# Attention of a graph network: a fourth probability chunk turned by DMA in heads 4 and 5, and the next tile's queries and mask fetched with heads 7, 0 to 3 and 5

## The chip, the cores and the metric

The kernel runs on one core of one Trainium2 chip. A core has TensorE (PE; its weight loads are listed as PEld), VectorE (DVE), ScalarE (ACT), GpSimd (POOL) and SyncE (SP), which here only issues DMAs. The metric is the time of one execution on the device, in microseconds; lower is better.

## What is computed

A graph convolution layer, then two transformer layers over the 2500 nodes, 40,000 edges, then a layer norm. The change lies in the attention of the two transformer layers:

```python
scores = jnp.einsum('ehd,ehd->eh', q[tgt], k[srcidx])
m = jax.ops.segment_max(scores, tgt, num_segments=n)
p = jnp.exp(scores - m[tgt])
s = jax.ops.segment_sum(p, tgt, num_segments=n)
w = p / (s[tgt] + 1e-16)
agg = jax.ops.segment_sum(w[:, :, None] * v[srcidx], tgt, num_segments=n)
attn = agg.reshape(n, D) @ Wo[l].T + bo[l]
x = _batchnorm(x + attn, g1[l], beta1[l])
```

n is 2500, D 512, with 8 heads of 64.

## The kernel before

The kernel does the sparse attention densely. A table `bias_rows` of 2500 x 2500 holds, for every pair of nodes, a mask or the logarithm of the number of edges, which is added to the score. The nodes are cut into 20 tiles of 125 target nodes. For each tile all 8 heads are worked, 160 units (tile, head) per layer, u = 8 * tile + head; the 2500 source nodes of a unit are 5 chunks of 500, k = 0 to 4.

For each chunk: PE makes the scores in PSUM (`score`, 2 matmuls of 500 columns, as the queries are kept in two fp16 halves). DVE adds the mask and keeps the chunk's maximum (`add_bias`); after five chunks it makes the unit's maximum (`maximum`, semaphore `maxed`). ACT takes the exponential in three pieces, chunks 0 and 1, chunks 2 and 3, chunk 4 (`exps`). Then the probabilities have to be turned so that source nodes lie on the partitions, and be cut into a high and a low fp16 half. There are two ways:

- By PE, chunks 1 and 3: 4 transposes in fp32 into a bank of `t_ps` (`turn_weights`), ACT copies the high half to `p_hi` (`high_half`), DVE subtracts to get `p_lo` (`low_half`).
- By DMA, chunks 0, 2 and 4 (`BY_DMA`): POOL (for chunk 4 ACT) copies the high half into a buffer `staged` (`high_to_stage`), POOL subtracts for the low half (`low_to_stage`), SP issues one DMA transpose of both halves into `across` (`turn`). There are 3 buffers `staged` (`STAGES`) and 4 `across` (`ACROSS`), used in the order of the chunks. A high half may be written only when the transpose of the chunk three before has landed (`crossed`), and a transpose may go out only when PE has used the chunk four before (`weighted`).

In both cases PE then multiplies with the values, 8 matmuls of 128 columns per chunk (`weigh`), three chunks behind the scores in its order. ACT and DVE read out the unit's sum (`read_high`, `read_low`).

The order of each engine is written out by hand, and each engine works it strictly in order. In its turn u of the loop PE does for k = 0 to 4: scores (u+2, k), transposes (u, k) if by PE, one piece of the tile's extra work (`EXTRA`), and `weigh` of the chunk three back. The extra work is that of the tile before: its sums transposed (heads 1 and 2) and the product with `wo`, two of four parts in head 3 and two in head 4. ACT does in turn u: `high_half(u, 1)`, `high_half(u, 3)`, `read_high(u-1)`, `exps(u+1, 0)` at k = 0, `(u+1, 1)` at k = 2, `(u+1, 2)` at k = 4, and right behind that `high_to_stage(u+1, 4)`. POOL goes through the DMA chunks only, and SP through their transposes. SP also fetches the next tile's 16-bit queries (two DMAs, one per half of the partitions, at head 0) and its mask (five chunks of columns, at heads 1 to 5), ahead of the transposes of the same head. DVE normalises the tile before at the end of its turn of head 0.

Of the kernel before, what the change touches and what calls it, by code (L numbers as in the profile page):

```python
# [86 lines left out]
ACROSS = 4  # L87

# [3 lines left out]
for u in range(UNITS):  # L92
    for k in range(NKC):
        if k in BY_PE:
# [1052 lines left out]
def attention(nc, sem, psum, sb, g, layer):  # L1147
# [6 lines left out]
    with ExitStack() as ctx:  # L1154
# [37 lines left out]
        high_staged = {k: sem(f"high_staged{k}") for k in BY_DMA}  # L1192
        low_staged = {k: sem(f"low_staged{k}") for k in BY_DMA}
# [15 lines left out]
        def pe_chunk(u, k):  # L1209
            return len(BY_PE) * (U0 + u) + BY_PE.index(k)  # L1210

        def dma_chunk(u, k):
            return len(BY_DMA) * (U0 + u) + BY_DMA.index(k)

        def dma_chunk_at(n):
            return n // len(BY_DMA), BY_DMA[n % len(BY_DMA)]

        def user_done(engine, n):

            if n < 0:  # L1220
                return
            in_layer, n = divmod(n, len(USERS))
            what, where, part = USERS[n]
            if what == "P":
                engine.wait_ge(bank_read, len(BY_PE) * (UNITS * in_layer + where) + BY_PE.index(part) + 1)
# [13 lines left out]
        def high_to_stage(engine, copy, u, k):  # L1239
            n = dma_chunk(u, k)  # L1240
            engine.wait_ge(stages_cleared, CLEARED * (layer + 1))
            if n >= STAGES:
                m = n - STAGES
                engine.wait_ge(crossed[m % ACROSS], 16 * (m // ACROSS + 1))
            apart(engine, g["waits_met"])
            for piece, (c0, c1) in enumerate(EXPS):
                if c0 <= k < c1:
                    engine.wait_ge(exped, len(EXPS) * (U0 + u) + piece + 1)
            copy(staged[n % STAGES][0:P, 0:BPC, 0:P],  # L1249
                 prob[u % PROBS][:, k * KC:(k + 1) * KC].rearrange("p (s c) -> p s c", s=BPC)).then_inc(high_staged[k], 1)  # L1250

        def low_to_stage(engine, u, k):
            here = staged[dma_chunk(u, k) % STAGES]
            engine.wait_ge(high_staged[k], U0 + u + 1)
            engine.tensor_tensor(here[0:P, BPC:2 * BPC, 0:P],  # L1255
                                 prob[u % PROBS][:, k * KC:(k + 1) * KC].rearrange("p (s c) -> p s c", s=BPC),
                                 here[0:P, 0:BPC, 0:P], ALU.subtract).then_inc(low_staged[k], 1)

        with nc.Block() as block:
            @block.sync  # L1260
            def _(sp):
                def load_queries(t):
                    for half in range(2):
                        sp.dma_start(queries_sb[t % 2][64 * half:64 * half + 64, 0:QW],
                                     q_tiles[t * DH:(t + 1) * DH, :]).then_inc(q_loaded[t % 2], 16)

                def load_mask(t, c):
                    at = slice(c * KC, (c + 1) * KC)
                    for p0, p1 in CUTS:
                        sp.dma_start(bias[t % 2][p0:p1, at], bias_rows[P * t + p0:P * t + p1, at]).then_inc(mask_loaded[t % 2], 16)  # L1270

                def turn(u, k):
                    n = dma_chunk(u, k)
                    if n >= ACROSS:
                        before, chunk = dma_chunk_at(n - ACROSS)
                        sp.wait_ge(weighted, NKC * before + chunk + 1)
                    sp.wait_ge(low_staged[k], U0 + u + 1)
                    apart(sp, g["waits_met"])
                    sp.dma_start_transpose(across[n % ACROSS][:, :, :], staged[n % STAGES][:, :, :].rearrange("p s c -> p (s c)")
                                           ).then_inc(crossed[n % ACROSS], 16)  # L1280

                load_queries(0)
                for c in range(NKC):
                    load_mask(0, c)
                for u in range(UNITS):
                    t, h = u // H + 1, u % H
                    if t < NT:

                        if h == 0:
                            if t > 1:  # L1290
                                sp.wait_ge(maxed, U0 + H * (t - 1))
                            load_queries(t)
                        if 0 < h <= NKC:
                            load_mask(t, h - 1)
                        if t == 1 and h == NKC + 1:
                            sp.dma_start(wo_sb[:, :, :].rearrange("p c d -> p (c d)"), g["wo"][layer * 128:(layer + 1) * 128, :]
                                         ).then_inc(wo_loaded, 16)
                    for k in BY_DMA:
                        turn(u, k)

            @block.gpsimd
            def _(pool):
# [7 lines left out]
                for u in range(UNITS):  # L1310
                    for k in BY_DMA:
                        if HIGH_BY[k] == "POOL":
                            high_to_stage(pool, pool.tensor_copy, u, k)
                        if LOW_BY[k] == "POOL":
                            low_to_stage(pool, u, k)

            @block.tensor
            def _(pe):
# [29 lines left out]
                def weigh(u, k):  # L1348
                    if k == 0:
                        reached(pe, agg_out, U0 + u - 1)  # L1350
                    if k in BY_PE:
# [44 lines left out]
                for u in range(UNITS):  # L1396
                    for k in range(NKC):
                        if u + 2 < UNITS:
                            score(u + 2, k)
                        if k in BY_PE:  # L1400
# [13 lines left out]
            def _(act):  # L1414
# [8 lines left out]
                def high_half(u, k):  # L1423
# [28 lines left out]
                for u in range(UNITS):  # L1452
                    for k in range(NKC):
                        if k in BY_PE:
# [15 lines left out]
            def _(dve):  # L1470
                def add_bias(u, c):
                    b = u // H % 2
                    if c == 0:
                        if u % H == 0:
                            dve.wait_ge(mask_loaded[b], BOTH * NKC * ((T0 + u // H) // 2 + 1))
                        for k in BY_DMA:
                            reached(dve, low_staged[k], U0 + u - PROBS + 1)
# [53 lines left out]
                def stage_lows(u, step):  # L1531

                    for k in BY_DMA:
                        if LOW_BY[k] == "DVE" and k + 2 == step:
                            low_to_stage(dve, u, k)

# [4 lines left out]
                for step in range(NKC):  # L1541
                    stage_lows(0, step)
                for u in range(UNITS):
                    for k in range(NKC):
                        if u + 2 < UNITS:
                            add_bias(u + 2, k)
                        if k in BY_PE:
# [324 lines left out]
```

## Time and profile before

| | us |
|---|---|
| median of 3 runs | 3387.66 |
| lowest, highest | 3385.79, 3404.86 |
| the profiled execution | 3393.12 |
| its span | 3391.3 |
| attention, layer 0 | about 1000 to 1962 |
| attention, layer 1 | about 2285 to 3245 |

The profile covers one execution. A line of the page or of a view says: line and engine, operation, what it writes and reads by the program's names (buffer numbers left out), shapes, count, busy time and mean ns of one, and the idle time ahead of it with what ended it. A timeline gives single instructions by start time. Matmuls are pipelined: one of 128 columns is shown with 0.22 us and the next starts 0.055 us later, so start times and not durations tell what PE spends.

### The profile page before, as it was taken

How to read it: one execution, taken by the hardware profiler on the slowest of the kernel's cores; microseconds unless marked ns; L12 is line 12 of the kernel's file. 1: busy time of each engine (PE TensorE's matmuls, PEld its weight loads, DVE VectorE, ACT ScalarE, POOL GpSimd, SP SyncE). 2: the span in 40 equal slices, each digit the busy share in tenths (PEclk: the TensorE clock that was granted, in tenths of full speed). 3: DMA queues.
4: the chain of work that ended last, by engine and by line, in shares of the span. 5: the costliest groups of instructions: out<-in, count | busy, mean ns of one | idle time of the engine just before them, and what ended most of it. 6: DMA issues, size and time to landing. Idle time of an engine off the chain costs nothing. (4 is left out here: it accounts for less than half of the span.)

```text
span 3391.3 us, 72342 instructions
## 1 busy us (share of the span) xinstructions
PE 2990.1 (88%) x24802; PEld 2279.6 (67%) x24802; DVE 2267.0 (67%) x6951; ACT 1965.5 (58%) x3918; POOL 2155.7 (64%) x1991
## 2 busy tenths in 40 slices
PE   2368999978869999999999989989999999999985
PEld 2124655645537778887787877757777778888874
DVE  8594334332337888888888853227888888888856
ACT  0123444433337788888787821227787788888834
POOL 1687877778617777777777710007777777777734
PEclk9999999988989999999999989999999999999998
DMA  9666666645579888888888831238898988888852
GB/s 372 102 126 157 125 122 130 114 91 92 99 194 171 168 166 170 170 175 175 162 167 174 156 84 25 52 72 177 166 166 166 174 171 171 168 173 173 162 120 61
DMA packets 1297462, 496.76 MB, mean 146 GB/s; under 512 B 1237240, under 2 KB 1262865, under 8 KB 1291408
## 3 DMA queue, kind: packets, MB, share of 16 engines
q1 hardware_dynamic: 1156197, 460.22, 63.7%
q0 software_dynamic: 133120, 0.80, 4.2%
q10 hardware_dynamic: 7788, 31.21, 2.8%
q8 instruction: 196, 3.21, 0.4%
q14 instruction: 161, 1.32, 0.1%
HBM read 153.55 MB, written 80.48 MB: 69 GB/s over the span
## 5 line engine op out<-in xcount | busy, mean ns | idle before, releaser
L1255 POOL TENSOR_TENSOR staged<-prob,staged 125x500 f16<-125x500 f32 x960 | 1071.3, 1122 | 166.0 <-ACT staged L1249 87.0
L1483 DVE CUSTOM_DVE_ANT_0 prob<-s_ps,mask 125x500 f32<-125x500 f32 x1600 | 1042.3, 673 | 179.5 <-PE s_ps L1333 116.2
L1420 ACT ACTIVATE prob<-prob,neg_max 125x1000 f32<-125x1000 f32 (+1 forms) x960 | 954.7, 994 | 58.9 <-DVE scrap L1489 53.8
L1333 PE MATMUL s_ps<-keys,queries 128*128 128x500 f16 x3200 | 945.7, 377 | 43.7 <-DMA queries<-q_tiles 28.0
L529 POOL DMA_INDIRECT counts<-count,cell x320 | 653.3, 2042 | 256.3 <-issue 98.1
L1361 PE MATMUL o_ps<-values,across 125*128 125x128 f16 x7680 | 586.8, 219 | 63.9 <-DMA across<-staged 63.4
L1361 PEld LDWEIGHTS o_ps<-values,across 125*128 125x128 f16 x7680 | 502.7, 97 | 200.8 <-issue 70.1
L1249 POOL CAST staged<-prob 125x500 f16<-125x500 f32 x640 | 385.5, 602 | 334.4 <-ACT prob L1420 201.6
L1496 DVE TENSOR_TENSOR p_lo<-t_ps,p_hi 125x500 f16<-125x500 f32 x640 | 434.4, 679 | 171.6 <-ACT p_hi L1430 167.2
L1430 ACT CAST p_hi<-t_ps 125x500 f16<-125x500 f32 x640 | 364.0, 569 | 146.3 <-PE t_ps L1344 145.0
L1344 PEld LDWEIGHTS t_ps<-identity,prob 125*125 125x125 f32 x2560 | 378.2, 188 | 92.0 <-ACT prob L1420 4.4
L1344 PE MATMUL t_ps<-identity,prob 125*125 125x125 f32 x2560 | 383.9, 272 | 2.7 <-ACT agg L1440 2.7
L1361 PE MATMUL o_ps<-values,p_hi 125*128 125x128 f16 x2560 | 355.6, 219 | 1.1 <-DVE p_lo L1496 1.1
L1361 PE MATMUL o_ps<-values,p_lo 125*128 125x128 f16 x2560 | 354.7, 219 | 0.0
L1249 ACT CAST staged<-prob 125x500 f16<-125x500 f32 x320 | 195.6, 611 | 202.9 <-issue 144.1
L1333 PEld LDWEIGHTS s_ps<-keys,queries 128*128 128x128 f16 x3200 | 249.7, 100 | 65.2 <-DVE chunk_max L1483 31.0
L1361 PEld LDWEIGHTS o_ps<-values,p_lo 125*128 125x128 f16 x2560 | 250.5, 98 | 26.8 <-issue 0.5
L1361 PEld LDWEIGHTS o_ps<-values,p_hi 125*128 125x128 f16 x2560 | 250.5, 98 | 25.8 <-DVE p_lo L1496 2.9
L1304 POOL MEMSET staged<- 128x1024 f16 x6 | 5.5, 951 | 381.0 <-POOLq L1053 307.8
L1383 PEld LDWEIGHTS t_ps<-agg,wo_sb 128*128 128x128 f32 x1280 | 169.9, 195 | 24.1 <-DVE p_lo L1496 2.1
L1420 ACT ACTIVATION_READ_ACCUMULATOR prob<-prob,neg_max 125x1 f32 x960 | 185.3, 193 | 0.0
L899 PE MATMUL agg_ps<-values,turned 125*125 125x512 f32 x400 | 180.9, 592 | 0.0
(162 smaller groups left out, 3684.2 us busy)
## 6 DMA issues: line engine op xcount, KB each, us to landing
mask<-bias_rows SPq DMA_DIRECT2D x200, 218.8 KB
counts<-xt ACTq DMA_DIRECT2D x8, 3054.0 KB, 37.2
keys<-counts SPq DMA_DIRECT2D x40, 546.9 KB
bias_rows<-edge_bias SPq DMA_DIRECT2D x20, 1093.8 KB
queries<-q_tiles SPq DMA_DIRECT2D x80, 250.0 KB, 3.9
pair_row<-pair_flat SPq DMA_DIRECT2D x40, 437.5 KB
across<-staged SPq DMA_TRANSPOSE x960, 3.0
q_tiles<-q_both SPq DMA_DIRECT2D x80, 125.0 KB, 3.0
```

What stands on the lines that cost most here:

```text
L529: pool.indirect_dma_start(counts, bass.IndirectOffsetOnAxis(cell[:, c:c + 1], 0), count[:, c:c + 1], None, compute_op=ALU.add).then_inc(gr ...
L899: mm = pe.matmul(agg_ps[t % 2][0:P, :], lhsT=turned_sb[u % 2][0:P, j * P:(j + 1) * P], rhs=hw(s), start=(s == 0), stop=(s == NT - 1))
L1249: copy(staged[n % STAGES][0:P, 0:BPC, 0:P], prob[u % PROBS][:, k * KC:(k + 1) * KC].rearrange("p (s c) -> p s c", s=BPC)).then_inc(high_st ...
L1255: engine.tensor_tensor(here[0:P, BPC:2 * BPC, 0:P], prob[u % PROBS][:, k * KC:(k + 1) * KC].rearrange("p (s c) -> p s c", s=BPC), here[0:P ...
L1333: mm = pe.matmul(s_ps[n % SB][:, 0:KC], lhsT=queries_sb[b][:, at:at + 128], rhs=keys[:, h, c * KC:(c + 1) * KC], start=(part == 0), stop=( ...
L1344: mm = pe.transpose(t_ps[r][0:P, s * P:(s + 1) * P], prob[u % PROBS][:, (k * BPC + s) * P:(k * BPC + s + 1) * P], identity[0:P, 0:P])
L1361: mm = pe.matmul(o_ps[u % 2][:, 0:2 * DH], lhsT=weights[:, s, :], rhs=values[:, u % H, k * BPC + s, :], start=(k == 0 and s == 0 and half ...
L1383: mm = pe.matmul(t_ps[r][:, 0:P], lhsT=wo_sb[:, k, o * 128:(o + 1) * 128], rhs=agg_t[t % 2][:, k * P:(k + 1) * P], start=(k == 0), stop=(k ...
L1420: act.activation(here, here, ACT.Exp, bias=neg_max[u % 4][:, :], accum_out=sums[u // H % 2][:, u % H, piece:piece + 1]).then_inc(exped, 1)
L1430: act.copy(p_hi[m % PB][:, :, 0:P], t_ps[r][0:P, 0:KC].rearrange("p (s c) -> p s c", s=BPC)).then_inc(p_high, 1)
L1483: dve.tensor_tensor_reduce(out=prob[u % PROBS][:, at], in0=s_ps[n % SB][0:P, 0:KC], in1=bias[b][:, at], scale=1.0, scalar=MASKED, op0=ALU. ...
L1496: dve.tensor_tensor(p_lo[m % PB][:, :, 0:P], t_ps[r][0:P, 0:KC].rearrange("p (s c) -> p s c", s=BPC), p_hi[m % PB][:, :, 0:P], ALU.subtrac ...
```

## The change

Heads 4 and 5 (`MORE_AT`) turn chunk 1 by DMA too, so that they have chunks 0, 1, 2 and 4 by DMA and only chunk 3 by PE. POOL makes both halves of chunk 1. The chunks are numbered through in two lists, `DMA_CHUNKS` and `PE_CHUNKS`, and the waits count by these; chunks 0 and 1 share one pair of semaphores. The number of buffers stays at 3 and 4. The next tile's fetches are spread anew: at head 7 of tile t, ahead of its transposes, SP waits for `maxed` and fetches the first half of the queries and mask chunk 0 of tile t + 2; then, in tile t + 1, the second half of the queries at head 0, mask chunks 1 to 3 at heads 1 to 3, and chunk 4 at head 5. The branch for low halves on DVE, which was not used, is gone. The core of the diff:

```diff
-BY_DMA = (0, 2, 4)
-BY_PE = tuple(k for k in range(NKC) if k not in BY_DMA)
-HIGH_BY = {0: "POOL", 2: "POOL", 4: "ACT"}
-LOW_BY = {0: "POOL", 2: "POOL", 4: "POOL"}
+MORE_AT = (4, 5)
+HIGH_BY = {0: "POOL", 1: "POOL", 2: "POOL", 4: "ACT"}
+STAGED_BY = {0: 0, 1: 0, 2: 2, 4: 4}
...
+def by_dma(u):
+    return (0, 1, 2, 4) if u % H in MORE_AT else (0, 2, 4)
...
                 def turn(u, k):
                     n = dma_chunk(u, k)
                     if n >= ACROSS:
-                        before, chunk = dma_chunk_at(n - ACROSS)
-                        sp.wait_ge(weighted, NKC * before + chunk + 1)
-                    sp.wait_ge(low_staged[k], U0 + u + 1)
+                        sp.wait_ge(weighted, weighted_by(DMA_CHUNKS, n - ACROSS))
+                    sp.wait_ge(low_staged[STAGED_BY[k]], staged_by(u, k))
...
-                load_queries(0)
+                def begin_next(t):
+                    if t < NT:
+                        if t > 1:
+                            sp.wait_ge(maxed, U0 + H * (t - 1))
+                        load_queries(t, 0)
+                        load_mask(t, 0)
+
+                def go_on(t, h):
+                    if t < NT:
+                        if h == 0:
+                            load_queries(t, 1)
+                        elif h <= 3:
+                            load_mask(t, h)
+                        elif h == 5:
+                            load_mask(t, 4)
+
+                for half in range(2):
+                    load_queries(0, half)
                 for c in range(NKC):
                     load_mask(0, c)
+                begin_next(1)
                 for u in range(UNITS):
-                    t, h = u // H + 1, u % H
-                    if t < NT:
-
-                        if h == 0:
-                            if t > 1:
-                                sp.wait_ge(maxed, U0 + H * (t - 1))
-                            load_queries(t)
-                        if 0 < h <= NKC:
-                            load_mask(t, h - 1)
-                        if t == 1 and h == NKC + 1:
...
-                    for k in BY_DMA:
+                    t, h = u // H, u % H
+                    if h == H - 1:
+                        begin_next(t + 2)
+                    else:
+                        go_on(t + 1, h)
+                    if t == 0 and h == NKC + 1:
...
+                    for k in by_dma(u):
                         turn(u, k)
```

## Rows read from the trace of the kernel before

**Rows 1.** Windows: stretch, us, busy (count) PE, PEld, DVE, ACT, POOL, PEclk, DMA share, GB/s.

```profile
1000.00:1962.00 962.00, 922.71 (x9867) 758.55 (x9865) 800.93 (x2579) 763.94 (x1625) 715.65 (x795) 0.99 0.85 167
2285.00:3245.00 960.00, 924.88 (x9934) 760.06 (x9934) 802.69 (x2586) 768.28 (x1637) 720.42 (x800) 1.00 0.86 168
1254.20:1302.04 47.84, 46.31 (x504) 38.37 (x502) 40.24 (x129) 38.83 (x83) 35.81 (x40) 1.00 0.88 172
1254.20:1260.88 6.68, 5.39 (x61) 4.26 (x59) 5.04 (x17) 5.10 (x12) 3.34 (x4) 1.00 1.10 217
...
1286.35:1291.58 5.23, 5.23 (x62) 4.24 (x60) 4.37 (x16) 4.06 (x9) 3.88 (x5) 1.00 0.72 131
```

**Rows 2.** Groups by line on PE, 1000 to 1962 us.

```profile
L1361 PE MATMUL o_ps<-values,across 125*128 125x128 f16 x3792 | 290.4, 219 | 33.4 <-DMA across<-staged 33.1
```

**Rows 3.** Timeline of PE: start us, us, line, out<-in, count; head 5 and later.

```profile
1289.82 0.60 PE L1344 MATMUL t_ps<-identity,prob 125*125 125x125 f32 x4
1290.26 0.61 PE L1361 MATMUL o_ps<-values,across 125*128 125x128 f16 x8
...
1293.31 0.22 PE L1361 MATMUL o_ps<-values,p_hi 125*128 125x128 f16 x1
...
1295.49 0.61 PE L1361 MATMUL o_ps<-values,across 125*128 125x128 f16 x8
...
1300.72 0.61 PE L1361 MATMUL o_ps<-values,across 125*128 125x128 f16 x8
...
1306.04 0.55 PE L1361 MATMUL o_ps<-values,across 125*128 125x128 f16 x7
```

**Rows 4.** Timeline of POOL, the same tile; in brackets the idle time before.

```profile
1277.15 0.60 POOL L1249 CAST staged<-prob 125x500 f16<-125x500 f32 x1 [1.93 <-ACT prob L1420]
1277.84 1.11 POOL L1255 TENSOR_TENSOR staged<-prob,staged 125x500 f16<-125x500 f32 x1
...
1281.95 0.60 POOL L1249 CAST staged<-prob 125x500 f16<-125x500 f32 x1 [0.22 <-issue]
...
1286.45 1.10 POOL L1255 TENSOR_TENSOR staged<-prob,staged 125x500 f16<-125x500 f32 x1 [0.98 <-ACT staged L1249]
1288.64 0.60 POOL L1249 CAST staged<-prob 125x500 f16<-125x500 f32 x1 [1.08 <-ACT prob L1420]
...
1294.56 1.11 POOL L1255 TENSOR_TENSOR staged<-prob,staged 125x500 f16<-125x500 f32 x1
```

**Rows 5.** Timeline of SP's DMA issues, the same tile (successive ones of a kind merged).

```profile
1279.02 4.31 SPq L1279 DMA_TRANSPOSE across<-staged  x3
1283.38 1.01 SPq L1270 DMA_DIRECT2D mask<-bias_rows  x2
...
1300.27 1.22 SPq L1264 DMA_DIRECT2D queries<-q_tiles  x2
```

**Rows 6.** Landing times of line L1279's transposes issued at 1279.0, 1284.5, 1301.7.

```profile
DMA to landing us min/median/max: 2.8/2.8/2.8
...
DMA to landing us min/median/max: 4.0/4.0/4.0
...
DMA to landing us min/median/max: 4.2/4.2/4.2
```

**Rows 7.** Timeline of ACT, the same tile.

```profile
1284.92 0.72 ACT L1420 ACTIVATE prob<-prob,neg_max 125x500 f32<-125x500 f32 x1
...
1285.77 0.61 ACT L1249 CAST staged<-prob 125x500 f16<-125x500 f32 x1
1286.72 1.13 ACT L1420 ACTIVATE prob<-prob,neg_max 125x1000 f32<-125x1000 f32 x1 [0.35 <-DVE scrap L1489]
...
1288.75 1.13 ACT L1420 ACTIVATE prob<-prob,neg_max 125x1000 f32<-125x1000 f32 x1
...
1290.46 0.58 ACT L1430 CAST p_hi<-t_ps 125x500 f16<-125x500 f32 x1 [0.49 <-PE t_ps L1344]
```

**Rows 8.** The page's groups, DVE's subtraction.

```profile
L1496 DVE TENSOR_TENSOR p_lo<-t_ps,p_hi 125x500 f16<-125x500 f32 x640 | 434.4, 679 | 171.6 <-ACT p_hi L1430 167.2
```

More of the change, by code:

```diff
@@ L87, with by_pe @@
 ACROSS = 4
+def by_dma(u):
+    return (0, 1, 2, 4) if u % H in MORE_AT else (0, 2, 4)
+def by_pe(u):
+    return tuple(k for k in range(NKC) if k not in by_dma(u))
+DMA_CHUNKS = [(u, k) for u in range(UNITS) for k in by_dma(u)]
+PE_CHUNKS = [(u, k) for u in range(UNITS) for k in by_pe(u)]
+DMA_AT = {chunk: n for n, chunk in enumerate(DMA_CHUNKS)}
+PE_AT = {chunk: n for n, chunk in enumerate(PE_CHUNKS)}
+STAGED_AT = {}
+for signal in (0, 2, 4):
+    for n, chunk in enumerate(c for c in DMA_CHUNKS if STAGED_BY[c[1]] == signal):
+        STAGED_AT[chunk] = n
+STAGED_COUNT = {signal: sum(STAGED_BY[k] == signal for u, k in DMA_CHUNKS) for signal in (0, 2, 4)}
 EXTRA = {(1, 4): ("T", 0), (2, 2): ("T", 1), (3, 2): ("O", 0), (3, 4): ("O", 1), (4, 2): ("O", 2), (4, 4): ("O", 3)}
@@ L93 @@
     for k in range(NKC):
-        if k in BY_PE:
+        if k in by_pe(u):
             USERS.append(("P", u, k))
@@ L1224, in user_done @@
             if what == "P":
-                engine.wait_ge(bank_read, len(BY_PE) * (UNITS * in_layer + where) + BY_PE.index(part) + 1)
+                engine.wait_ge(bank_read, len(PE_CHUNKS) * in_layer + PE_AT[where, part] + 1)
             elif what == "T":
@@ L1261, in _, with load_queries @@
             def _(sp):
[L1262 to L1265, printed above, removed]
+                def load_queries(t, half):
+                    sp.dma_start(queries_sb[t % 2][64 * half:64 * half + 64, 0:QW],
+                                 q_tiles[t * DH:(t + 1) * DH, :]).then_inc(q_loaded[t % 2], 16)
                 def load_mask(t, c):
@@ L1310, in _ @@
                 for u in range(UNITS):
-                    for k in BY_DMA:
+                    for k in by_dma(u):
                         if HIGH_BY[k] == "POOL":
                             high_to_stage(pool, pool.tensor_copy, u, k)
-                        if LOW_BY[k] == "POOL":
-                            low_to_stage(pool, u, k)
+                        low_to_stage(pool, u, k)
             @block.tensor
@@ L1475, in add_bias @@
                             dve.wait_ge(mask_loaded[b], BOTH * NKC * ((T0 + u // H) // 2 + 1))
-                        for k in BY_DMA:
-                            reached(dve, low_staged[k], U0 + u - PROBS + 1)
+                        if u >= PROBS:
+                            for k in by_dma(u - PROBS):
+                                dve.wait_ge(low_staged[STAGED_BY[k]], staged_by(u - PROBS, k))
+                        elif layer > 0:
+                            for signal in STAGED_COUNT:
+                                dve.wait_ge(low_staged[signal], STAGED_COUNT[signal] * layer)
                         apart(dve, g["waits_met"])
@@ L1529, in statistics @@
                                      xt[:, o, c * CH:(c + 1) * CH]).then_inc(bn_chunks, 1)
[L1531 to L1535, printed above, removed]
                 for u in range(2):
```

44 lines of the change are left out of this document (21 added, 23 removed).

## The prediction

> **Notation.** Chunk (h,k) is columns 500k to 500k+499 of head h's probabilities; (8,0) is head 0 of the next tile. A "unit" is one turn of the loop over heads. Times within the tile are written without their leading 1,2 or 1,3: 77.15 is 1277.15 us, 102.9 is 1302.9 us.
>
> **What bounds the kernel now.** I read first the busy times by stretch. The two attention stages hold 1922 us of the 3391 us span, and in them TensorE (PE) is busy 923 of 962 and 925 of 960 us, at the full granted clock [rows 1]. One tile of 8 heads takes 47.84 us with PE busy 46.31; nothing else in it comes near (DVE 40.24, ACT 38.83, POOL 35.81) [rows 1]. Then PE by line: of layer 0's idle time 33.4 us lie ahead of products with `across`, for 33.1 us of which the landing of a turned chunk is waited for [rows 2]. The windows say where: head 0 of the tile has 5.39 us of PE work in 6.68 us [rows 1], the rest being the wait for (0,0). So PE is the bound, and a second thing sits right behind it: the ring POOL copy, POOL subtract, SP issue, DMA landing, which has three `staged` buffers.
>
> How tight that ring is, the timeline of the engines in the tile 1254.20 to 1302.04 tells. A POOL chunk costs 0.60 + 1.11 us, with gaps 1.79 us from first start to end: 77.15, 77.84 + 1.11 = 78.95 [rows 4]. SP issues at 79.02 and needs about 1.3 us per transpose [rows 5]. It lands 2.8 us later when no fetch is near, 4.0 us later behind a mask's fetch, 4.2 us behind the queries' [rows 6]. A buffer's cycle is thus 1.79 + 0.08 + 2.8 + 0.14 = 4.8 us at best, for three chunks, against 5.23 us of PE time in a head without the product [rows 1].
>
> **Part 1: what is taken from PE.** In heads 4 and 5 the four fp32 transposes of chunk 1 go. They take 89.82 to 90.26 = 0.44 us of PE [rows 3]. Two per tile, 40 tiles: 80 x 0.44 = 35 us. The 8 products of the chunk stay, with `across` in place of `p_hi`/`p_lo`, at the same pitch. ACT loses one copy of 0.58 us, DVE one subtraction of 679 ns [rows 7, 8] per head, neither of which sets PE's time there: worth nothing by themselves.
>
> **Part 2: what is added.** Per such head POOL gets 1.79 us, SP one transpose of 1.3 us, the ring one more chunk. PE's shortening makes it worse: after both heads PE asks 0.88 us sooner. I follow the tile step by step, with the same durations.
> - (4,0): copy at 77.15 as now, subtracted 78.95, issued 79.0, landed 81.8.
> - (4,1), new: POOL 79.0 to 80.8. (4,2): to 82.7, issued 82.8, landed 85.6.
> - (4,4): ACT makes its high half, into the buffer of the chunk three before. That was (3,4), landed long ago; it is now (4,0), so ACT is held until 81.8 + 0.14 = 81.95 and its exponentials of head 5 end at 83.7 and 84.9. ACT has room here: it is waiting for PE anyway in this long unit, and exp (5,2) ends at 86.3 instead of 85.64 [rows 7]. POOL's half of (4,4) ends at 83.9, and SP may issue it at 84.1.
> - (5,0): POOL 83.95 to 85.75 (now 81.95 + 1.79 = 83.74 [rows 4]). SP: 84.1 + 1.23 + 1.01 for the mask of head 5 [rows 5] = 86.35; issue 86.4. It lands at 90.4 with the 4.0 us of its own row, at 89.2 with 2.8 us. PE reaches it at 90.26 - 0.88 = 89.4 [rows 3]: a stall of 0 to 1.0 us.
> - (5,4): ACT's high half stands in its queue ahead of the exponentials of head 6. The chunk three before is now (5,0), not (4,4). So ACT, which copies at 85.77 today [rows 7], is held until 89.35 to 90.55. Queued behind it: exp (6,0) and (6,1) at 1.13 us each and the copy of (5,3) at 0.58 us [rows 7], then DVE's subtraction at 0.68 us [rows 8]. Sum: 0.61 + 1.13 + 1.13 + 0.58 + 0.68 = 4.1 us, so `p_lo` of (5,3) is there at 93.5 to 94.7. PE wants it today at 93.31 [rows 3] and would after the change at 92.4. **Here the 0.88 us won are gone, and PE is 0.2 to 1.5 us later than today**, exp (6,0) at 91.1 to 92.3 against 87.85 is 3.2 to 4.4 us later.
>
> This hold is the step that I weigh most. DVE's bias adds and the next maximum also stand behind that subtraction.
>
> **Part 3: the fetches moved.** Mask 0 and half of the queries now stand ahead of (7,0) in SP's queue (1.01 + 0.6 us [rows 5]); the other half stays ahead of (8,0), which saves 0.6 us of issue there and some of the 4.2 us landing. The wait for `maxed` moved with them is for head 7's maximum, which ACT's exponentials needed before (7,0) could be staged: nothing, and queued behind it on SP is only (7,0). Head 4 is free of its mask (1.01 us of SP), which (4,0) uses. For the moved fetch alone: today (7,0) leaves POOL at 95.67 [rows 4], lands 4.0 us after its issue (as long as (5,0)'s) [rows 6], so at 99.7, and is reached at 100.72 [rows 3]: 1 us to spare; 1.6 us more of SP eats that, and (8,0) then waits for the buffer of (7,0). Gain and loss are about even.
>
> Together: exp (6,0) late by 3.2 to 4.4 us sets POOL to (6,0) at 91.2 to 92.4 instead of 88.64 [rows 4]; POOL then runs without a break, (6,0), (6,2), its half of (6,4), and ends (7,0) at 97.8 to 99.1. SP issues (6,4) at 96.0 to 97.5, then the fetch: (7,0) goes out at 98.9 to 100.4, lands at 101.7 (2.8 us) to 104.6 (4.2 us). PE gets it 1.1 to 4.0 us later than 100.72. (8,0) takes its buffer: +0.14 + 1.79 + 0.08 + 2.8 to 3.6 us of landing = 106.6 to 110.3, against 106.04 today [rows 3]. **One tile: +0.6 to +4.3 us.** I take +3.1, nearer the upper end, since (5,0) has the mask just ahead of it as its 4.0 us row has, and (7,0) a fetch as large as the one of the 4.2 us row; off the end, as each PE stall gives POOL and ACT time. With 38 tiles that have both parts: 38 x 3.1 = +118 us.
>
> The Trainium skill, Perfetto Trace Analysis, Optimization Strategy, says that the same gap repeating on the engine that should be full can mean too few buffers; the 33.1 us of waits for `across`, most of them for (0,0), agree. By it a fourth chunk in a three-buffer ring costs rather than saves; it gives no figure of its own.
>
> **The sum.** The profiled execution took 3393.1 us (span 3391.3), 5.5 above the median 3387.66. 3393 + 118 = 3511, on the median's scale 3505 us.
>
> **The rivals.**
> 1. *The relief is paid out (faster).* ACT's hold is short because (5,0) lands earlier than I say: it decides at 85.7, when ACT comes to the copy today; every landing before about 88.5 leaves (5,3) on time. Then 35 us are won, and if halving the queries' fetch also ends the waits for (0,0), at most 33 us per layer [rows 2], of which DVE at 40.24 of 47.84 us lets perhaps half through: 3388 - 35 - 30 = 3323, or 3353 without it. For it: PE is busiest by far. Against it: POOL has six full chunks and two halves to do between 77.15 and (5,4)'s end. Chance 0.15. The Trainium skill, Perfetto Trace Analysis, Identifying the Most-Contended Engine, would have the busiest engine relieved first, and so sides with this.
> 2. *POOL alone matters (even).* ACT's hold hides in PE's waits, and only POOL's 3.6 us per tile tell, of which its idle time today before (5,4) and (6,0) (0.98 + 1.08 us [rows 4]) takes 2.1. The remaining 1.5 us and PE's 0.88 stand against 2.2 us by which (6,0) is early today (POOL ends it at 88.64 + 1.79 = 90.43 [rows 4], landed 93.3 with 2.8 us, reached at 95.49 [rows 3]); the fetch ahead of (7,0) takes the gain back. -0.9 to +0.9 us per tile, centre 3390. Chance 0.22.
> 3. *The forecast*, chance 0.63, own range 3411 (+0.6) to 3551 (+4.3).
>
> **From cases to numbers.** A measurement of this kernel tells about 1% from no change: bounds 3354 and 3422. Faster: rival 1 with few exceptions, 0.15. Within 1%: rival 2 and the forecast's lowest edge, 0.23. Slower: 0.62. The range runs from 3370 (cutting off rival 1's 0.15) to 3560.
>
> **What would show it.** In the changed trace: POOL busy up by 80 x 1.7 = 137 us, transposes x1040, PE's t_ps<-identity,prob x2240. ACT's idle time ahead of `staged` on ACT, with (5,0)'s landing as what ends it, some 4 us per tile in head 5: the hold. PE then waits for DVE `p_lo` (today 0) and for `across` in heads 7 and 0. I am wrong in Part 2 if ACT's copy of (5,4) starts within 2 us of the end of exp (5,2), and in Part 3 if (7,0) lands in under 3.2 us.

## The result and the profile after

| | us |
|---|---|
| median of 3 runs | 3519.86 |
| lowest, highest | 3510.33, 3522.35 |
| the profiled execution, its span | 3510.33, 3508.1 |
| ratio to before, 95% interval | 1.0382 [1.0354, 1.0409] |

The change makes the kernel slower by 132 us, 3.8%. The page of the changed kernel, its busy times and three groups (columns as before: count, then busy us and mean ns, then the idle time just ahead and what ended it):

```profile
PE 2998.6 (85%) x24482; PEld 2234.0 (64%) x24482; DVE 2221.0 (63%) x6871; ACT 1901.7 (54%) x3838; POOL 2280.7 (65%) x2151
...
L1397 PE MATMUL o_ps<-values,across 125*128 125x128 f16 x8320 | 638.4, 219 | 148.1 <-DMA across<-staged 146.5
...
L1380 PE MATMUL t_ps<-identity,prob 125*125 125x125 f32 x2240 | 337.1, 273 | 3.7 <-ACT agg L1475 3.5
...
L1274 ACT CAST staged<-prob 125x500 f16<-125x500 f32 x320 | 195.6, 611 | 493.6 <-issue 434.0
```

The fp32 transposes are gone as meant (2240), and the 640 products moved to `across` are there (8320). But the wait for `across` has grown: 146.5 us in the whole span, where the kernel before has 63.4 (33.1 of it in layer 0, [rows 2]). ACT's copies into `staged` show the same thing: ACT stood idle ahead of them for 434.0 us of "issue", against 144.1 before. "Issue" is idle time for which the view names no releaser; in the tile below such a wait ends just behind the landing that frees the buffer.

```profile
L1249 ACT CAST staged<-prob 125x500 f16<-125x500 f32 x320 | 195.6, 611 | 202.9 <-issue 144.1
```

Of the 116.8 us by which the span grew, PE's waits for a landing take 83.1, those for DVE's maximum 22.5 (15.5 to 38.0), those for `p_lo` 9.5 (1.1 to 10.6): 115 us. PE's busy time should have fallen by 35 us and rose by 8.5. Part of that is how a busy PE is counted: eight products that stand alone are shown with 0.61 us [rows 3], while in a row they take 8 x 0.055 = 0.44, so every wait costs about 0.17 us more than the idle time shown; 140 more waits of these three kinds make 24 us. The other 20 us are open.

**Where it happens** is read from the windows of one tile, 1352.26 to 1403.36, here the whole tile and its heads 4, 5, 6 and 7 (columns as in [rows 1]):

```profile
1352.26:1403.36 51.10, 46.81 (x495) 37.09 (x493) 38.52 (x127) 36.76 (x80) 39.33 (x45) 1.00 0.89 171
1377.30:1383.87 6.57, 6.57 (x74) 5.67 (x72) 3.95 (x16) 4.01 (x9) 4.84 (x6) 1.00 0.71 141
1383.87:1388.84 4.97, 4.96 (x57) 3.66 (x55) 3.85 (x16) 1.47 (x4) 3.54 (x5) 1.00 0.84 193
1388.84:1396.06 7.22, 6.20 (x62) 4.08 (x59) 4.10 (x14) 6.31 (x15) 6.57 (x9) 1.00 0.68 141
1396.06:1403.36 7.30, 5.57 (x59) 4.27 (x59) 5.69 (x19) 5.73 (x14) 4.00 (x6) 1.00 1.14 205
```

The same four heads of before:

```profile
1279.34:1286.35 7.01, 7.01 (x78) 6.19 (x75) 5.05 (x16) 5.40 (x11) 5.67 (x7) 1.00 0.89 195
1286.35:1291.58 5.23, 5.23 (x62) 4.24 (x60) 4.37 (x16) 4.06 (x9) 3.88 (x5) 1.00 0.72 131
1291.58:1296.81 5.23, 5.23 (x62) 4.24 (x60) 4.73 (x16) 4.81 (x11) 4.45 (x6) 1.00 0.75 155
1296.81:1302.04 5.23, 5.23 (x62) 4.25 (x60) 4.64 (x16) 4.81 (x11) 3.81 (x5) 1.00 1.07 163
```

Head 4 wins exactly its 0.44 us (7.01 to 6.57). Head 5 wins 0.26. Then heads 6 and 7, which the change leaves alone but for the fetch, lose 1.99 and 2.07 us. Heads 0 to 3 take 25.04 us against 25.14. So the tile is 3.26 us longer (51.10 against 47.84), and all of its loss lies in heads 6 and 7, behind the change. The granted clock is full on both sides.

One tile is one case. The averages of 36 tiles of each trace (18 per layer, without the first and the last; a head is counted from its first matmul of scores to that of the next head) say how far it is typical, in us. The runs e1 to e9 are described below:

| | 0 | 1 | 2 | 3 | 4 | 5 | 6 | 7 | tile |
|---|---|---|---|---|---|---|---|---|---|
| before | 6.21 | 6.04 | 5.57 | 7.40 | 7.01 | 5.23 | 5.23 | 5.30 | 48.00 |
| the change | 5.60 | 6.43 | 5.75 | 7.14 | 6.57 | 5.56 | 7.12 | 6.89 | 51.05 |
| e1_fetch_only | 5.34 | 6.67 | 5.54 | 7.19 | 7.01 | 5.23 | 5.23 | 6.26 | 48.48 |
| e2_chunk_only | 7.16 | 5.90 | 5.83 | 7.12 | 6.58 | 5.79 | 7.13 | 5.66 | 51.17 |
| e4_before_4buf | 5.72 | 6.13 | 5.44 | 7.06 | 7.00 | 5.23 | 5.23 | 5.23 | 47.05 |
| e3_after_4buf | 5.52 | 6.29 | 5.45 | 7.02 | 6.57 | 5.01 | 5.95 | 6.34 | 48.15 |
| e9_less7 | 5.26 | 6.88 | 5.53 | 7.11 | 7.00 | 5.23 | 5.23 | 5.66 | 47.91 |

The tile shown is typical in heads 4, 6 and 7. In head 5 it is a lucky one: on average that head loses 0.33 us.

ACT in that tile, heads 4 and 5 (idle time before in brackets):

```profile
1379.86 0.61 ACT L1274 CAST staged<-prob 125x500 f16<-125x500 f32 x1 [3.18 <-issue]
...
1383.17 0.71 ACT L1456 ACTIVATE prob<-prob,neg_max 125x500 f32<-125x500 f32 x1
...
1387.47 0.61 ACT L1274 CAST staged<-prob 125x500 f16<-125x500 f32 x1 [3.50 <-issue]
1387.99 1.12 ACT L1456 ACTIVATE prob<-prob,neg_max 125x1000 f32<-125x1000 f32 x1
...
1390.22 0.55 ACT L1465 CAST p_hi<-t_ps 125x500 f16<-125x500 f32 x1
```

SP, which sends the transposes and the moved fetches:

```profile
1395.66 0.58 SPq L1288 DMA_DIRECT2D queries<-q_tiles  x1
1396.29 1.02 SPq L1294 DMA_DIRECT2D mask<-bias_rows  x2
1397.44 4.10 SPq L1302 DMA_TRANSPOSE across<-staged  x3
```

And PE:

```profile
1389.76 0.62 PE L1397 MATMUL o_ps<-values,across 125*128 125x128 f16 x8 [0.33 <-DMA across<-staged]
...
1391.55 0.23 PE L1397 MATMUL o_ps<-values,p_hi 125*128 125x128 f16 x1 [0.31 <-DVE p_lo L1535]
...
1402.05 0.61 PE L1397 MATMUL o_ps<-values,across 125*128 125x128 f16 x8 [1.71 <-DMA across<-staged]
```

ACT comes to the copy of (5,4) at 1383.97 and gets its buffer at 1387.47, 0.11 us after the landing of (5,0) (issued 1384.16, 3.2 us). Queued behind it are the exponentials of head 6 and the high half of (5,3), so PE gets `p_lo` of (5,3) late at 1391.55. POOL starts on head 6 late, at 1389.27, and then has only one break, of 0.40 us, before (7,0). SP sends (7,0) behind the fetch at 1397.44, it lands 4.5 us later, and PE stands 1.71 us for it.

### The profile page after: what moved, and what is told of

It reads as the page before. It is cut to its first block and busy times, and to the rows that moved or that the text cites. A ratio compares the mean times of both kernels' runs of the same rounds, so it can differ in the third digit from the quotient of the medians.

```text
span 3508.1 us, 71820 instructions
## 1 busy us (share of the span) xinstructions
PE 2998.6 (85%) x24482; PEld 2234.0 (64%) x24482; DVE 2221.0 (63%) x6871; ACT 1901.7 (54%) x3838; POOL 2280.7 (65%) x2151
## 5 line engine op out<-in xcount | busy, mean ns | idle before, releaser
L1280 POOL TENSOR_TENSOR staged<-prob,staged 125x500 f16<-125x500 f32 x1040 | 1149.9, 1110 | 214.4 <-ACT staged L1274 129.7
L1397 PE MATMUL o_ps<-values,across 125*128 125x128 f16 x8320 | 638.4, 219 | 148.1 <-DMA across<-staged 146.5
L1397 PEld LDWEIGHTS o_ps<-values,across 125*128 125x128 f16 x8320 | 537.3, 98 | 323.0 <-issue 118.5
L1274 POOL CAST staged<-prob 125x500 f16<-125x500 f32 x720 | 434.8, 604 | 287.1 <-ACT prob L1456 186.0
L1535 DVE TENSOR_TENSOR p_lo<-t_ps,p_hi 125x500 f16<-125x500 f32 x560 | 380.1, 679 | 307.2 <-ACT p_hi L1465 306.1
L1274 ACT CAST staged<-prob 125x500 f16<-125x500 f32 x320 | 195.6, 611 | 493.6 <-issue 434.0
L1380 PEld LDWEIGHTS t_ps<-identity,prob 125*125 125x125 f32 x2240 | 331.7, 188 | 82.8 <-ACT prob L1456 5.9
L1465 ACT CAST p_hi<-t_ps 125x500 f16<-125x500 f32 x560 | 315.9, 564 | 61.5 <-PE t_ps L1380 60.4
L1380 PE MATMUL t_ps<-identity,prob 125*125 125x125 f32 x2240 | 337.1, 273 | 3.7 <-ACT agg L1475 3.5
L1397 PE MATMUL o_ps<-values,p_hi 125*128 125x128 f16 x2240 | 312.6, 220 | 11.3 <-DVE p_lo L1535 10.6
L1397 PE MATMUL o_ps<-values,p_lo 125*128 125x128 f16 x2240 | 311.3, 219 | 0.0
```

The costliest lines, as they stand in the source:

```text
L1274: copy(staged[n % STAGES][0:P, 0:BPC, 0:P], prob[u % PROBS][:, k * KC:(k + 1) * KC].rearrange("p (s c) -> p s c", s=BPC)).then_inc(high_st ...
L1280: engine.tensor_tensor(here[0:P, BPC:2 * BPC, 0:P], prob[u % PROBS][:, k * KC:(k + 1) * KC].rearrange("p (s c) -> p s c", s=BPC), here[0:P ...
L1380: mm = pe.transpose(t_ps[r][0:P, s * P:(s + 1) * P], prob[u % PROBS][:, (k * BPC + s) * P:(k * BPC + s + 1) * P], identity[0:P, 0:P])
L1397: mm = pe.matmul(o_ps[u % 2][:, 0:2 * DH], lhsT=weights[:, s, :], rhs=values[:, u % H, k * BPC + s, :], start=(k == 0 and s == 0 and half ...
L1465: act.copy(p_hi[m % PB][:, :, 0:P], t_ps[r][0:P, 0:KC].rearrange("p (s c) -> p s c", s=BPC)).then_inc(p_high, 1)
L1535: dve.tensor_tensor(p_lo[m % PB][:, :, 0:P], t_ps[r][0:P, 0:KC].rearrange("p (s c) -> p s c", s=BPC), p_hi[m % PB][:, :, 0:P], ALU.subtrac ...
```

## The experiments

A ratio is always to the kernel before on the same chip; there that kernel took 3374 to 3378 us, and 3387.66 in the first row. The column "buffers" gives those of `staged`. "Old fetches" in an edit means SP's fetches as in the kernel before:

```diff
-                begin_next(1)
...
-                    if h == H - 1:
-                        begin_next(t + 2)
-                    else:
-                        go_on(t + 1, h)
+                    if t + 1 < NT:
+                        if h == 0:
+                            if t > 0:
+                                sp.wait_ge(maxed, U0 + H * t)
+                            load_queries(t + 1, 0)
+                            load_queries(t + 1, 1)
+                        if 0 < h <= NKC:
+                            load_mask(t + 1, h - 1)
```

| run | chunks by DMA per tile | buffers, fetches | us | ratio [95%] |
|---|---|---|---|---|
| the change | 26 | 3, new | 3519.86 | 1.0382 [1.0354, 1.0409] |
| e1_fetch_only | 24 | 3, new | 3407.57 | 1.0095 [1.0072, 1.0119] |
| e2_chunk_only | 26 | 3, old | 3519.95 | 1.0419 [1.0399, 1.0439] |
| e5_act_later | 26 | 3, new | 3525.75 | 1.0444 [1.0421, 1.0466] |
| e3_after_4buf | 26 | 4, new | 3395.79 | 1.0066 [1.0043, 1.0089] |
| e4_before_4buf | 24 | 4, old | 3347.20 | 0.9919 [0.9887, 0.9951] |
| e6_no_pool | 26 | 3, new | 3524.88 | 1.0449 [1.0419, 1.0480] |
| e7_stage4_across3 | 24 | 4 (`across` 3), old | 3385.57 | 1.0027 [1.0012, 1.0042] |
| e8_one_head | 25 | 3, old | 3452.33 | 1.0227 [1.0197, 1.0256] |
| e9_less7 | 23 | 3, old | 3385.49 | 1.0035 [1.0023, 1.0046] |
| e10_less7_newfetch | 23 | 3, new | 3407.35 | 1.0094 [1.0080, 1.0108] |
| e11_less0 | 23 | 3, old | 3416.77 | 1.0115 [1.0100, 1.0130] |
| e12_moved_chunk | 24 | 3, old | 3435.22 | 1.0166 [1.0148, 1.0184] |

### The two parts apart

e1_fetch_only, an edit to the changed kernel:

```diff
-MORE_AT = (4, 5)
+MORE_AT = ()
```

> The changed kernel with three DMA chunks in every head again; only the fetches stand where the change put them. Theory (ACT held at head 5's last chunk is the main loss, the moved fetch is about even by itself, since (7,0) had 1 us to spare and (0,0) gains what (7,0) loses): 3360 to 3410 us, ratio to before within 1%; PE's wait for the turned chunk moves from head 0 to head 7. Rival A (the fetch ahead of head 7 is the main loss, 1.6 us of PE waiting per tile there in the changed kernel): 3440 us or more. Rival B (the fetch move is a gain that the fourth chunk spoils): 3355 us or less.

e2_chunk_only is the changed kernel with the old fetches.

> The changed kernel with the queries and mask fetched at heads 0 to 5 as before; only the fourth chunk stays. Theory: the loss in heads 5 and 6 stays whole (PE idle 2.7 us there against 0.04), that of head 7 shrinks from 1.7 us to some 0.5, head 0's wait of 1 us comes back: +1 to +2 us per tile, 3425 to 3470 us. Rival A (the fetch is the main loss): 3355 to 3400 us, the relief of 35 us on PE showing at least in part. Additive effects would need e1 + e2 to sum to the change's +132 us; if they sum to less, the two make each other worse.

The fetch alone costs 0.95%, 31 us, and the chunks alone 4.2%: as much as both together. e2 is a miss; I had left a share of 50 to 90 us to the fetch. The groups of PE and the windows of a head 7 and the head 0 behind it in e1 tell what the fetch does:

```profile
L1397 PE MATMUL o_ps<-values,across 125*128 125x128 f16 x7680 | 587.9, 219 | 70.9 <-DMA across<-staged 69.9
L1369 PE MATMUL s_ps<-keys,queries 128*128 128x500 f16 x3200 | 945.4, 377 | 52.0 <-DMA queries<-q_tiles 27.0 <-DVE chunk_max L1522 24.4
...
2967.38:2973.38 6.00, 5.40 (x62) 4.26 (x60) 4.75 (x17) 4.87 (x12) 2.93 (x4) 1.00 1.08 237
2973.38:2978.60 5.22, 5.22 (x61) 4.24 (x59) 4.48 (x15) 4.43 (x9) 4.88 (x6) 1.00 0.70 170
```

Head 0, which took 6.68 us [rows 1], is down to 5.22. Head 7 is up from 5.23 to 6.00. The stall has moved from (8,0) to (7,0), and these two heads together lose nothing: on average head 7 is 0.96 us longer and head 0 is 0.87 shorter. What the fetch costs shows in head 1, which is 0.63 us longer. PE's waits altogether grew by 6.5 us for `across` and by 8.9 for DVE's maximum; these 15 us are half of the 31.

### Who is held: ACT, POOL or the ring

e5_act_later takes ACT's copy of (4,4) and (5,4) out of the way of the exponentials:

```diff
-                        if HIGH_BY[k] == "ACT" and step == min(k // 2 * 2 + 1, NKC - 1):
+                        if HIGH_BY[k] == "ACT" and u % H not in MORE_AT and step == min(k // 2 * 2 + 1, NKC - 1):
                             high_to_stage(act, act.copy, u, k)
...
+                        if k == 2 and u % H in MORE_AT:
+                            high_to_stage(act, act.copy, u, 4)
```

> The changed kernel, but in heads 4 and 5 ACT makes the high half of chunk 4 two steps later, behind the first two exponentials of the next head instead of ahead of them. No work or buffer is changed. Theory (the hold in ACT's queue): exponential (6,0) ends some 3 us earlier, PE's waits for p_lo and for DVE in head 6 (0.9 us per tile) go, and part of the wait in head 7: 1 to 2 us per tile, 3445 to 3480 us. Rival (POOL and the three-buffer ring by themselves bound heads 5 to 7, ACT's hold runs alongside): 3505 to 3530 us.

It gained nothing (1.0444). Its ACT timeline tells why, the copies of (5,4) and of (6,4):

```profile
3253.56 1.13 ACT L1456 ACTIVATE prob<-prob,neg_max 125x1000 f32<-125x1000 f32 x1 [0.99 <-DVE scrap L1530]
...
3256.66 0.61 ACT L1274 CAST staged<-prob 125x500 f16<-125x500 f32 x1 [0.76 <-ACT prob L1456]
...
3262.03 0.61 ACT L1274 CAST staged<-prob 125x500 f16<-125x500 f32 x1 [3.47 <-issue]
```

and its POOL timeline:

```profile
3257.35 1.10 POOL L1280 TENSOR_TENSOR staged<-prob,staged 125x500 f16<-125x500 f32 x1 [1.14 <-ACT staged L1274]
3258.39 0.60 POOL L1274 CAST staged<-prob 125x500 f16<-125x500 f32 x1
```

The exponential (6,0) is now done at 3254.69, as early as I wanted. But POOL takes up (6,0) only at 3258.39, since it makes its half of (5,4) first, and that waits for the same buffer: (5,0) lands at 3256.57, ACT copies (5,4) at 3256.66 and POOL follows at 3257.35. In head 6 ACT is held for 3.47 us, the hold of the changed kernel one head later. PE's waits for `across` stay (148.5 us). So the run does not free ACT everywhere (its idle time of "issue" ahead of `staged` is 318.9 us, against 434.0). What it shows is that an early exponential (6,0) alone gains nothing, since POOL then waits for the same buffer in its own queue.

e6_no_pool takes the new chunk's work from POOL: high half by ACT, low half by DVE.

```diff
-HIGH_BY = {0: "POOL", 1: "POOL", 2: "POOL", 4: "ACT"}
-STAGED_BY = {0: 0, 1: 0, 2: 2, 4: 4}
+HIGH_BY = {0: "POOL", 1: "ACT", 2: "POOL", 4: "ACT"}
+LOW_BY = {0: "POOL", 1: "DVE", 2: "POOL", 4: "POOL"}
+STAGED_BY = {0: 0, 1: 1, 2: 2, 4: 4}
...
-                        low_to_stage(pool, u, k)
+                        if LOW_BY[k] == "POOL":
+                            low_to_stage(pool, u, k)
...
-                        if HIGH_BY[k] == "ACT" and step == min(k // 2 * 2 + 1, NKC - 1):
+                        if HIGH_BY[k] == "ACT" and step == (3 if k == 1 else min(k // 2 * 2 + 1, NKC - 1)):
...
+                        if k == NKC - 1 and u + 1 < UNITS and 1 in by_dma(u + 1):
+                            low_to_stage(dve, u + 1, 1)
```

> The changed kernel, but chunk 1 of heads 4 and 5 gets its high half from ACT and its low half from DVE, which both have room there, so that POOL does what it did before the change; the three buffers and the order of the transposes stay. Ring theory (a buffer comes free only when the transpose three chunks before has landed, four chunks per head turn it 8 times in two heads): (4,4) still waits for (4,0) and (5,4) for (5,0), 0.2 to 0.5 us per tile better at most, 3490 to 3525 us. POOL theory (its 3.6 us more per tile): 3390 to 3430 us.

Its page:

```profile
PE 3001.3 (85%) x24482; PEld 2235.7 (64%) x24482; DVE 2270.3 (65%) x6951; ACT 1945.0 (55%) x3918; POOL 2165.9 (62%) x1991
```

POOL is back near its 2156 us of before (2165.9), and the time is 3524.88, so POOL's own work is not what costs. In e6 ACT and DVE have more to do, so some gain could be hidden there; e3, next, leaves POOL all of its added work and still recovers most. e3_after_4buf and e4_before_4buf give the ring a fourth buffer. Memory for it comes from `wo_sb`: both load only three quarters of `wo` and use the third quarter's columns in place of the fourth, so PE does the same work, with another output.

```diff
-STAGES = 3
+STAGES = 4
...
-        wo_sb = sb(ctx, "wo_sb", [128, FC, D])
+        wo_sb = sb(ctx, "wo_sb", [128, FC, 384])
...
-                        mm = pe.matmul(t_ps[r][:, 0:P], lhsT=wo_sb[:, k, o * 128:(o + 1) * 128],
+                        mm = pe.matmul(t_ps[r][:, 0:P], lhsT=wo_sb[:, k, min(o, 2) * 128:(min(o, 2) + 1) * 128],
```

> The changed kernel with four staged buffers instead of three. To make room in SBUF only three quarters of wo are kept, and the fourth part of the product uses the third part's columns: same work on every engine, another output. Theory (the ring, by the hold and by POOL's own waits): ACT's copy of (5,4) waits for (4,4) instead of (5,0), POOL's copies no longer wait for a landing: 3400 to 3450 us, POOL busy the same. Rival (POOL's own 1.79 us per chunk, SP's issues and the landings bound it, the buffers don't): 3490 us or more.

> The kernel before with four staged buffers; three quarters of wo are kept and the fourth part of the product uses the third part's columns, as in e3_after_4buf: same work, another output. It is the fair base for that run. If the ring of buffers is also what makes PE wait in heads 0 and 3 today (1.4 us per tile), 3320 to 3360 us, and the changed kernel with four buffers (3396) is then slower than its own base: the fourth chunk and the fetches lose even without the ring. If the waits there are POOL's, SP's and the fetches' own time: within 12 us of before, and the two kernels with four buffers differ by under 1%.

The changed kernel falls from 1.0382 to 1.0066, the kernel before from 1 to 0.9919. The waits of PE for a landing in the two (whole span: us in total, times, longest), e3 first:

```profile
PE o_ps L1397 <- DMA across<-staged: 86.7, 102, 3.9
```

```profile
PE o_ps L1361 <- DMA across<-staged: 31.9, 48, 1.9
```

Without the fourth buffer they are 146.5 and 63.4. These are the runs that decide: the number of buffers `staged` carries most of the loss. The fourth buffer removes ACT's hold as well (65.1 us of "issue" in e3), so e3 alone does not tell the hold from the ring; e5 does, for (6,0). A limit of the DMA engines is ruled out too: in e3 they are busy 0.91 of the time and move 177 GB/s (1010 to 1970 us), in the changed kernel 0.85 and 168 (995 to 2018 us), so they had room.

The buffers don't carry all: with four of them the change still costs 48.6 us (3395.79 less 3347.20) where 35 us of PE work are gone. By the averages above it loses this in heads 6 and 7, at waits for `across` again (86.7 us against 31.9). Whether POOL, SP or the fetch makes them was not taken apart.

e7_stage4_across3 has the same memory as before, moved: `STAGES` 4 and `ACROSS` 3 in the kernel before.

```diff
-STAGES = 3
-ACROSS = 4
+STAGES = 4
+ACROSS = 3
```

> The kernel before with the eight buffers shared out 4 staged and 3 across instead of 3 and 4, its output unchanged. If the staged ring holds the chain today and the across ring has room, 3340 to 3375 us. If a transpose then waits for the product three chunks before (issue at that product's end, 3 us landing, reached 5.2 us later: 1 to 2 us to spare in a plain head, less beside a fetch), 3385 to 3430 us.

1.0027, or 3385.57 us: the lowest edge of the second expectation (3385 to 3430), with 72.9 us of waits for `across` against 63.4 and 9.8 for DVE against 15.5. What a fourth `staged` wins when `across` keeps its four (e4) is lost again when `across` gives one up.

### What one chunk costs, and whether one fewer pays

e8_one_head, with the old fetches:

```diff
-MORE_AT = (4, 5)
+MORE_AT = (4,)
```

> The old fetches and the fourth DMA chunk in head 4 alone. Half the dose: 17 us of PE relieved. If the loss were one fixed price per extra chunk, half of e2's +143 us, so 3440 to 3455 us. Ring theory: one extra chunk is largely covered by the 2.4 to 4 us of slack that head 4 has, the second one finds it used up, so far less than half: 3370 to 3410 us.

3452.33: a miss for the theory that one chunk fits into the slack of a tile, and in the range of a fixed price. One chunk per tile more costs (3452.33 - 3377.95) / 40 = 1.86 us, two cost (3519.95 - 3376.4) / 80 = 1.79 us each. A buffer's cycle at its best, 1.79 + 0.08 + 2.8 + 0.14 us, over three buffers is 1.6 us. So **from 24 chunks upwards, with three buffers, each added chunk costs about the ring's price**, although it takes 0.44 us from PE. The price holds for adding only: the runs below, with 23 chunks and with 24 placed otherwise, do not follow the number. And it is not simply divided by four with a fourth buffer: that would be 1.2 us, but there the two chunks and the fetch cost 48.6 / 80 = 0.61 us a chunk. POOL's time per chunk, 1.79 us, is as close to the measured price as the ring's 1.6; it is e3 and e6, and not the nearness of a number, that speak for the ring.

If so, a chunk fewer should win. e9_less7 gives chunk 4 of head 7 to PE (old fetches); e10_less7_newfetch is the same with the new ones.

```diff
-    return (0, 1, 2, 4) if u % H in MORE_AT else (0, 2, 4)
+    return (0, 2) if u % H == 7 else (0, 2, 4)
```

> The change's opposite, with the fetches of before: head 7 turns chunks 0 and 2 by DMA and chunk 4 by PE, no head has four by DMA. Per tile 23 chunks pass the ring instead of 24; PE gets 0.44 us of transposes, POOL loses 1.11 us, ACT swaps one copy for another, DVE gets 0.68 us. Measured so far: 24, 25 and 26 chunks took 47.9, 49.6 and 51.1 us per tile, 1.6 us each, a third of the 4.8 us in which a staged buffer is used again, and PE's relief did not show. If the ring sets the tile at 24 too, 23 give 0.5 to 1.2 us per tile back after PE's 0.44: 3335 to 3365 us, PE's wait at head 0 mostly gone. If PE is the bound at 24 and the ring only from 25 on, PE's 17 us show: 3385 to 3400 us.

> As e9_less7, with the fetches of the changed kernel (mask 0 and half of the queries ahead of head 7's transposes). Head 7 now has a transpose less (1.3 us of SP), about what the fetch there costs SP (1.6 us). Ring theory: the fetch, which cost 31 us alone, costs less than 15 us against e9_less7 or nothing. Otherwise the same 31 us as before.

e11_less0 takes it from head 0, where PE waits in the kernel before; e12_moved_chunk takes it from head 7 and gives head 0 a fourth, so that the ring has 24 again (both old fetches):

```diff
-    return (0, 1, 2, 4) if u % H in MORE_AT else (0, 2, 4)
+    return (0, 2) if u % H == 0 else (0, 2, 4)
...
-    return (0, 1, 2, 4) if u % H in MORE_AT else (0, 2, 4)
+    return (0, 2) if u % H == 7 else (0, 1, 2, 4) if u % H == 0 else (0, 2, 4)
```

> As e9_less7, but head 0 is the one with two DMA chunks. The chunk is taken from the ring behind (0,0), at whose landing PE waits, so that wait stays; it helps heads 1 and 3 (0.5 us per tile of waits for the ring) and adds 0.68 us to DVE where DVE is already late (PE waits 0.4 us for it in head 1). Ring theory: little or no gain, 3375 to 3400 us. If only the count of chunks per tile mattered and not the place: as e9_less7.

> As e9_less7 (head 7: two DMA chunks; fetches of before), and head 0 takes the chunk: 0, 1, 2 and 4 by DMA. Per tile 24 chunks again, PE's work as before. In e9_less7 the ring's waits were gone, but DVE, late after it has normalised the tile before, held PE's scores in head 1 for 1.4 us per tile instead of 0.4. Here head 0 costs DVE one subtraction (0.68 us) less just ahead of that. If DVE is what took e9_less7's gain: its wait in head 1 falls to 0.7 us or less, and as the chunks had 1.2 to 2.2 us to spare in heads 0 to 2, the ring comes back with 0.5 us or so: 47.2 to 47.5 us per tile, 3345 to 3365 us, faster than before. If the added ring slot costs its 1.6 us in full as in e8_one_head: 3400 us or more.

All four missed what the ring alone would give. e9 came out at the edge of the other reading (3385 to 3400, PE alone the limit), e12 in the range of a full price for the added chunk (3400 or more). e10 is between its two: the new fetch costs 21.9 us there, not under 15 and not 31. The waits of e9:

```profile
PE s_ps L1372 <- DVE chunk_max L1525: 52.4, 41, 3.2
...
PE o_ps L1400 <- DMA across<-staged: 20.5, 26, 4.7
```

The ring's waits are down from 63.4 to 20.5 us, as expected, but DVE's are up from 15.5 to 52.4, and PE has 40 x 0.44 = 18 us more to do. Its DVE in a head 1:

```profile
2962.14 1.31 DVE L1557 TENSOR_TENSOR agg<-agg,inverse 125x512 f32<-125x512 f32 x1
2963.38 0.67 DVE L1525 CUSTOM_DVE_ANT_0 prob<-s_ps,mask 125x500 f32<-125x500 f32 x1
...
2964.11 0.60 PE L1372 MATMUL s_ps<-keys,queries 128*128 128x500 f16 x2 [1.27 <-DVE chunk_max L1525]
```

and the same place of before:

```profile
1262.25 1.39 DVE L1515 TENSOR_TENSOR agg<-agg,inverse 125x512 f32<-125x512 f32 x1
1263.56 0.67 DVE L1483 CUSTOM_DVE_ANT_0 prob<-s_ps,mask 125x500 f32<-125x500 f32 x1
...
1264.29 0.60 PE L1333 MATMUL s_ps<-keys,queries 128*128 128x500 f16 x2 [0.19 <-DVE chunk_max L1483]
```

Head 1 starts at 2959.62 in e9 and at 1260.88 before. DVE normalises the last tile (1.3 us) and only then adds the bias of (3,0), 3.76 us after that start in e9 and 2.68 before. PE has come sooner and waits 1.27 us instead of 0.19: what (0,0) gave back in head 0 is taken in head 1. On average heads 0 and 1 together take 12.25 us before, 12.14 in e9 and 12.01 in e1: a stall taken from head 0 comes back in head 1.

e12 has these waits too (49.9 us) although its ring is as full as before, so the place of a chunk counts and not only the number. e11, with one chunk fewer in the very head that waited, is slower than e9 (3416.77 against 3385.49). PE's waits tell why: those for `across` are 47.0 us against 20.5 in e9, those for DVE 56.9 against 52.4, together 31.0 of the 31.3 us. So in e11 the ring still holds (0,0), and DVE is late all the same; why it is late there, where head 0 is no shorter, is open. In e12 the waits for `across` (49.7 us) and for `p_lo` (7.6 against 2.5) are 34 us above e9's, those for DVE 2.5 below, of 49.7 us lost. The new fetch costs 21.9 us between e9 and e10 and 31 in e1, so most of its price stays where the ring has room; 16.5 of the 21.9 are PE's waits for `across` (37.0 against 20.5).

No kernel with the whole computation beat the kernel before.

## Why the prediction came out

- **What bounds the kernel.** "PE is the bound, and a second thing sits right behind it" put the two in the wrong order for this change. PE is nearly full, yet taking 35 us from it brings none (e2), and e4, which adds only a buffer, wins 0.8%. The Trainium skill (Perfetto Trace Analysis, Optimization Strategy), cited in the prediction for too few buffers, agrees with e4. The prediction let the same page of the Trainium skill (Identifying the Most-Contended Engine) speak for rival 1. That is weaker than it looks: this section has the most-contended engine optimised first, but says that TensorE's headroom is to be judged by its share of peak arithmetic (MFU) and by its weight loads, not by matmul busy time. By the weight loads PE (PEld 38.37 us of 47.84) stands behind DVE (40.24) [rows 1]. By the runs, relieving PE at the ring's expense is 4.2% slower (e2).
- **Part 1.** Right: x2240 transposes, POOL up by 125 us (137 forecast), 0.44 us won in head 4.
- **Part 2, step by step.** Counted from the tile's start (1254.20 before, 1352.26 after): ACT's copy of (5,4) was forecast 35.2 to 36.4 us in, it came 35.2 in; exp (6,0) was to end 3.2 to 4.4 us later than before, it ends 36.9 in against 33.7, 3.2 later; `p_lo` of (5,3) was to be there 39.3 to 40.5 in, PE takes it 39.3 in; the landing of (5,0) 2.8 to 4.0 us, 3.2 measured. Each step came, and all but the last at the early end of its range. The hold of ACT, 3.2 and 3.5 us in heads 4 and 5, was forecast at some 4 us in head 5.
- **The step that failed** is the weight given to it: "This hold is the step that I weigh most." PE's waits for `p_lo` have grown by 9.5 us, those for `across` by 83. The waits for `across` alone do not refute the hold, since the prediction lets it reach (7,0) through the late exponential (6,0) and POOL. e5 does: there that exponential is on time, POOL takes up (6,0) late all the same, and nothing is gained. The hold is how the missing buffer shows in ACT's queue, not the cause. The ring arithmetic in the first paragraph (4.8 us for three chunks) already held the right cause and nearly the right size; I used it to describe the kernel and then summed delays of one path instead. That this sum came out is partly luck: ACT's hold and POOL's wait end with the same landing, that of (5,0), so either path gives nearly the same delay.
- **Part 3.** "About even" is right for heads 7 and 0 together (0.96 us lost, 0.87 won on average), but the fetch alone costs 31 us (e1), and the prediction did not look at head 1, where on average 0.63 us are lost. Beside the chunks the fetch adds nothing (e2 against the change): without it the loss of head 7 falls on head 0 instead (7.16 us against 5.60). (7,0) went out 45.2 us into the tile (44.7 to 46.2 forecast); that it would land in 2.8 to 4.2 us was a little low (4.5). It is open why the two prices do not add; that in the changed kernel SP's fetch falls into time in which the ring is late anyway is only argued.
- **The sum.** +3.1 us per tile was taken, +3.26 measured in the tile shown, 132.2 / 40 = 3.3 over all, 3.05 by the averages of the traces; of a range of +0.6 to +4.3. Counted from the tile's start, PE reached (7,0) 49.79 us in, against 46.52 before, 3.3 later (1.1 to 4.0 forecast), and (8,0), at 1407.44, 3.3 later (0.6 to 4.3). The forecast was 3505 us, measured 3519.86: right in sign and nearly in size.
- **The rivals.** The paid-out relief fails even with a fourth buffer (1.0066 against 0.9919). POOL's time alone fails by e6 and e3 together.

## What to carry to other kernels

Where a chain of copy, DMA and use goes round a few buffers, divide the cycle of one buffer by their number before moving work into it. Where the busy engine already waits for landings here and there, as PE does before the change (63.4 us), count on paying it for each further item (1.6 us by the rows here, 1.8 to 1.9 measured), even if the engine relieved is 97% busy. Don't count on getting it back for an item taken out: e9 got nothing. When a wait for a buffer stands ahead of other work in an in-order queue, moving it to another place tests little (e5); add a buffer to test, even at the cost of leaving work out. When a stall is removed, look at which engine's work is due next: here PE waited for DVE, which was still normalising the tile before, and what the ring gave was gone.

## What the runs showed of the hardware that I had not expected

- The landing of one transpose of the same size took 2.8 us with nothing near it [rows 6], 3.2 us for (5,0), and 4.5 us for (7,0) right behind two fetches. That the fetches make the difference is not shown: before the change (7,0), issued at 1295.7 with no fetch ahead of it in SP's queue [rows 5], took 4.0 us. The two landings of the changed kernel, by issue time:

```profile
DMA to landing us min/median/max: 3.2/3.2/3.2
...
DMA to landing us min/median/max: 4.5/4.5/4.5
```

- Each stall of PE costs some 0.17 us beside the idle time that the view shows (0.61 against 0.44 us for eight products), so a sum of waits understates what they cost when there are many short ones. This is a matter of how the view counts busy time.
